# Cross attention with quads of heads: the previous head's last weighing first, its value load ahead of GpSimd's maximum, and the second value product of a quad handled one step later

## What is computed

```python
q = (layernorm(x) @ Wq).reshape(b, sq, 16, 128) / sqrt(128)   # sq = 256
k = (ctx @ Wk).reshape(b, 4096, 16, 128)
v = (ctx @ Wv).reshape(b, 4096, 16, 128)
attn = softmax(einsum('bqhd,bkhd->bhqk', q, k), axis=-1)
x = x + einsum('bhqk,bkhd->bqhd', attn, v).reshape(b, sq, 2048) @ Wo
```

## Time and profile before

| what | value |
|---|---|
| median of 3 runs | 1631.89 us (1631.61 to 1635.02) |
| profiled execution: its own time | 1632.26 us |
| its span, first to last instruction | 1630.4 us |
| PE busy | 1595.6 us (98%) |
| DVE busy | 1175.9 us (72%) |
| ACT busy | 728.2 us (45%) |
| cross attention, about | the first 1155 us |

### The profile page before, as it was taken

The page is one execution under the profiler, slowest core; times in us unless marked ns, Lnnn a source line. Parts: engine busy times, 40 slices in busy tenths (PEclk is TensorE's granted clock), DMA queues, the critical chain, the costliest instruction groups (busy, mean ns, idle before and its releaser), DMA issues. The chain is left out here.

```text
span 1630.4 us, 23096 instructions
## 1 busy us (share of the span) xinstructions
PE 1595.6 (98%) x8798; PEld 1255.8 (77%) x8798; DVE 1175.9 (72%) x2127; ACT 728.2 (45%) x981; POOL 192.5 (12%) x247
## 2 busy tenths in 40 slices
PE   9999999999999999989999999998999999999998
PEld 7887888888788888878888888887757757544544
DVE  5555888888788888878888889999583762633333
ACT  4334554555455555544555556565331351322221
POOL 0001011010100101010110101111100071011110
PEclk9999999999999999999999999999999999999999
DMA  7876555564655655554455444334320517489994
GB/s 237 228 228 191 156 148 148 145 162 124 176 145 148 154 144 156 124 167 133 133 135 134 134 120 123 104 116 138 128 102 30 206 52 309 179 262 416 424 423 171
DMA packets 125661, 283.48 MB, mean 174 GB/s; under 512 B 7729, under 2 KB 83697, under 8 KB 119409
## 3 DMA queue, kind: packets, MB, share of 16 engines
q1 hardware_dynamic: 103248, 201.27, 38.1%
q0 software_dynamic: 22304, 80.75, 17.8%
HBM read 207.51 MB, written 74.48 MB: 173 GB/s over the span
## 5 line engine op out<-in xcount | busy, mean ns | idle before, releaser
L502 PE MATMUL bank<-wv_parts,cT_hi 128*128 128x512 f32 x1024 | 334.4, 390 | 1.0 <-DMA wv_parts<-wv_dram 1.0
L502 PEld LDWEIGHTS bank<-wv_parts,cT_hi 128*128 128x128 f32 x1024 | 192.8, 188 | 41.3 <-DMA wv_parts<-wv_dram 1.4
L470 PE MATMUL bank<-cT_hi,wk_hi 128*128 128x512 f32 x512 | 201.2, 393 | 0.6 <-DVE cT_lo L858 0.6
L470 PE MATMUL bank<-cT_lo,wk_hi 128*128 128x512 f32 x512 | 200.0, 391 | 0.0
L502 PE MATMUL bank<-wv_parts,cT_lo 128*128 128x512 f32 x512 | 199.8, 390 | 0.0
L470 PE MATMUL bank<-cT_hi,wk_lo 128*128 128x512 f32 x512 | 199.8, 390 | 0.0
L704 ACT CAST e_parts<-S 128x1024 fp32r<-128x1024 f32 (+1 forms) x129 | 134.9, 1045 | 139.7 <-PE bank L526 133.9
L964 DVE TENSOR_TENSOR e_parts<-S,e_parts 128x1024 fp32r<-128x1024 f32 (+1 forms) x129 | 156.0, 1209 | 40.6 <-ACT e_parts L704 37.7
L695 ACT ACTIVATE S<-S 128x1024 f32<-128x1024 f32 (+1 forms) x129 | 136.0, 1055 | 103.4 <-DVE S L930 101.3
L881 DVE TENSOR_TENSOR mx<-mx,S 128x256 f32<-128x256 f32 x390 | 165.3, 424 | 18.4 <-ACT S L689 8.1
L930 DVE TENSOR_TENSOR S<-S,mrow 128x1024 f32<-128x1024 f32 (+1 forms) x129 | 162.2, 1258 | 4.7 <-POOL mrow L1205 4.6
(11 more groups left out here) (328 smaller groups left out, 2793.7 us busy)
## 6 DMA issues: line engine op xcount, KB each, us to landing
w<-in_w_moe SPq DMA_DIRECT2D x32, 2304.0 KB, 15.4
v_dram<-v_out SPq DMA_DIRECT2D x112, 512.0 KB, 4.7
v_back<-v_dram POOLq DMA_DIRECT2D x110, 512.0 KB, 4.6
ctx_nat<-in_ctx SPq DMA_DIRECT2D x8, 1024.0 KB, 5.4
ctx_raw<-in_ctxT SPq DMA_DIRECT2D x7, 1024.0 KB, 8.9
v_dram<-v_back SPq DMA_DIRECT2D x14, 512.0 KB, 4.9
v_late<-v_dram POOLq DMA_DIRECT2D x14, 512.0 KB, 3.7
wv_parts<-wv_dram POOLq DMA_DIRECT2D x6, 1024.0 KB, 8.2
```

The source lines that it names most:

```text
L470: t = e.matmul(banks[b][:], l, r, start=(c == 0 and m == 0), stop=(c == DT - 1 and m == 2))
L502: t = e.matmul(banks[b][:], l, r, start=(c == 0 and m == 0), stop=(c == DT - 1 and m == 2))
```

## The change

It has four parts.

1. TensorE: in heads 4 and 8, step 0, `weigh(h-1, 7)` stands ahead of `project_k(h+1, 0)`, as in the other heads. GpSimd: in the same place `load_v` is issued ahead of `largest_score`.
2. ACT, DVE and SP: in the first head of each quad (0, 4 and 8) the second of step 1's two value units is rounded, subtracted and written at step 2, ahead of step 2's own. TensorE projects it where it did.
3. Heads 12 and 13: the weights of the queries are rounded and subtracted before those of the keys.
4. Head 14, step 6: `split_e` of the last chunk stands ahead of `keep_max` on DVE.

```diff
+        def moved_units(h, j):
+
+            if h < LATE and starts_quad(h) and j in (1, 2):
+                pair = units(h, 1)
+                return pair[:1] if j == 1 else pair[1:] + units(h, 2)
+            return units(h, j)
...
-                    for u in units(h, j):
+                    for u in moved_units(h, j):
                         spill(u)
...
-                    elif j == 0 and h and not starts_quad(h):
+                    elif j == 0 and h:
                         weigh(h - 1, NCH - 1)
                     project_k(h + 1, j)
-                    if j == 0 and h and starts_quad(h):
-                        weigh(h - 1, NCH - 1)
...
-                    for u in units(h, j):
+                    for u in moved_units(h, j):
                         round_v(u)
...
                     if j + 1 == NCH - 1 and h + 2 < XH:
+                        round_qo("wq", h + 2)
                         round_wk(h + 2)
-                        round_qo("wq", h + 2)
...
-                for u in units(h, 1):
+                for u in moved_units(h, 1):
                     split_v(u)
...
-                    for u in units(h, j):
+                    for u in moved_units(h, j):
                         split_v(u)
...
+                    if j == NCH - 2 and h == XH - 2:
+                        split_e(h, j + 1)
                     keep_max(h + 1, j - 1)
                     if j + 1 < NCH:
-                        split_e(h, j + 1)
+                        if j < NCH - 2 or h < XH - 2:
+                            split_e(h, j + 1)
...
                     if j + 1 == NCH - 1 and h + 2 < XH:
+                        split_qo("wq", h + 2)
                         split_wk(h + 2)
-                        split_qo("wq", h + 2)
...
                     if h < LATE:
-                        if h and j == 0 and starts_quad(h):
-                            largest_score(h)
                         load_v(n)
...
-                    if h and j == 0 and n != TAIL and not (h < LATE and starts_quad(h)):
+                    if h and j == 0 and n != TAIL:
                         largest_score(h)
```

## The result

The changed kernel took 1639.32 us (median of 6 runs, 1637.06 to 1639.88), the kernel before 1631.95 us on the same chip (6 runs, 1631.19 to 1635.02). The ratio is 1.0038, with a 95% interval from 1.0028 to 1.0048: slower by 6.2 us by the ratio, by 7.4 by the medians. The prediction was 1635.6, with a range of 1629.0 to 1641.0. The direction and the range are right, and the middle is 3.7 us too low.

The account below looks back on a forecast made before the run. TensorE, busy 98% of the span, was taken as the bound. Terms: +5.6 (heads 4 and 8), 0 (head 0), 0 (values), -1.5 (clock), -0.4 (parts 3 and 4), sum +3.7, giving 1635.6 us, range 1629.0 to 1641.0.

Parts of the forecast that it names:

- Part 2's waits: Step 3: TensorE waits 3.0 us in heads 4 and 8, about 2 in head 0; net loss 5.6 in heads 4 and 8.
- Rival A: The moved unit's write is hidden, ACT's wait is off TensorE's path: faster, 1627.7 us; chance 0.13.
- rival C: Clock falls in step 3's new waits, heads 4 and 8, 1.6 us each: clearly slower, 1638.8 us; chance 0.20.
- nearer to 2.25: Head 8's start: 2.5 us of idleness is nearer to head 4's 2.25 than to 3.91, so the clock holds.
- Net 0: Head 0: the 1.81 us wait is won in step 2 and lost in step 3; up to 1.9 lost with a longer write.
- I take a gain of 0: Start of heads 4 and 8: earlier load of values wins 0 us; the other end is 2.9 for both.
- an earlier issue only lengthens the stay in the queue: Start of head 8: values issued up to 2.7 us earlier still land behind the weights, at 706.2.
- cannot pass: GpSimd's queue: descriptors start in order, so the values cannot pass the weights and the gain is 0.
- Bare waits: Step 0 of heads 4 and 8: TensorE stands 1.57 us before the scores, where it stood 0.15; cost 1.4.
- the clock at head 8's start: Idleness comes in two pieces, 1.6 and 2.5 us, so the clock holds: gain about 1.5 us (0 to 1.6).
- -0.4: Heads 12 to 14, parts 3 and 4: gain of 0.4 us of a possible 1.0, all from part 3; other end 0.
- rival B: Early load lands early, full value of part 1 (2.9 us): no change, 1632.7 us; chance 0.17.

Follow-up runs that it names:

- Run 5: Changed kernel with the moved value unit written twice, first to a spare place in memory; 1645.46 us, ratio 1.0084 against the kernel before.
- run 3: Changed kernel with the second unit rounded and subtracted at the head of step 2, behind the exponential parts; 1624.85 us, ratio 0.9965 against before.
- Run 1: Changed kernel without part 2, each value unit handled in the step that projects it; 1627.03 us, ratio 0.9975 against the kernel before.
- run 2: Kernel before with part 2 alone, the second value unit handled at step 2; 1644.25 us, ratio 1.0076 against the kernel before.
- run 4: Kernel before with only TensorE's order of part 1, GpSimd's maximum still ahead of the load; 1629.0 us, ratio 0.9989 against before.
- Run 6: Kernel before with TensorE's order of part 1, head 8's key weights loaded behind step 1's writes; 1627.1 us, ratio 0.9972 against before.
- run 9: Kernel before with only GpSimd's order of part 1, load of values ahead of the maximum; 1633.38 us, ratio 1.0006 against before.
- run 7: Kernel before with parts 3 and 4 alone; 1632.98 us, ratio 1.0004 against the kernel before.
- run 8: Changed kernel without parts 3 and 4, the second unit handled at the head of step 2; 1625.05 us, ratio 0.9953 against the kernel before.

## Why the prediction was right in direction and short in size

**Part 2's waits: right.** The working gave 3.0 us in heads 4 and 8 and 2.0 in head 0, and 2.71, 2.85 and 2.25 came. Its steps held one by one in head 4: a write of 3.7 (3.67), the third unit at 444.5 (446.62, of which some 2.0 had been lost earlier), 5.7 from there to the keys of step 3 (452.30 - 446.62 = 5.68). ACT stood 5.02 us before that unit, where I had said about 4. (438.4 + 1.8 + 0.7 is 440.9 and not 440.7, which changes nothing.) Run 5 shows that the write's length goes through to TensorE, run 3 that the wait goes with the place and not with the step. Rival A falls with them.

**The clock behind them: the step that failed.** The sum counts the waits of part 2 at their own length. The fall was priced, at 1.6 us each, but only as rival C and for two heads. In the profiled execution it came behind all three waits: +4.8 us, which is more than the whole miss of 3.7. For head 8's start I had taken it that 2.5 us of idleness is "nearer to 2.25" and holds the clock, and used the same row of head 4 for the waits of step 3. The length of one wait does not decide: in the changed kernel's head 0 the clock fell after 2.25 us, the very length after which it had held before. "Net 0" for head 0 failed for this reason: the wait was moved and became dearer. The 0.69 that rival C quotes after 3.4 us is the mean of a window in which the clock fell from 1.00 to 0.50 on the way, so it was as full a fall as the others.

**The values' landing: mis-sized in head 8.** "I take a gain of 0" stood on the queue being full from the issue on, though the rows show landings and not how full a queue is. In the changed kernel the start of head 8 came 2.3 us earlier, the bound that I had worked out from the exponential parts; in head 4 it came 0.2 earlier. Run 1 has 2.25 and 3.91 us of waiting turned into 1.40 and 0.24 each. The times from issue to landing, counted from the start of the weights' row in GpSimd's timeline, are these (us; head 4 / head 8):

| kernel | values issued | values landed |
|---|---|---|
| before | 7.2 / 7.0 | 13.3 / 15.0 |
| run 2 | 7.2 / 7.0 | 13.3 / 14.5 |
| run 4 | 5.7 / 5.7 | 12.7 / 14.6 |
| changed kernel | 4.4 / 4.3 | 13.2 / 12.4 |
| run 1 | 4.4 / 4.3 | 12.4 / 12.8 |
| run 3 | 4.4 / 4.3 | 12.5 / 12.5 |

The changed kernel's issues in heads 4 and 8, as in the earlier trace rows:

```profile
v_back<-v_dram POOLq DMA_DIRECT2D x1, 512.0 KB, 8.7
...
v_back<-v_dram POOLq DMA_DIRECT2D x1, 512.0 KB, 8.1
```

So "an earlier issue only lengthens the stay in the queue" was nearly true in head 4, where an issue 2.7 us earlier landed 0.2 to 1.0 earlier. It was false in head 8, where the same landed 2.3 to 2.6 earlier, while the first 1.3 us of it (run 4) won only 0.4. The rule of the Trainium skill that I had set beside it (DMA: Bandwidth & Descriptors, section Two DMAs through the same engine are not ordered: descriptors of one queue start in order) agrees with the changed kernel, where the second transfer of weights landed at about 708.0 us (issued at some 698.4, 9.6 us to landing) and the values at 710.1. But start order is all that the page gives; that the values "cannot pass" and so gain 0 was my own step. They never did pass: they landed behind the weights in every trace that has both landings. Yet the weights' landing was not fixed either: it came 10.3 us behind the start of their row in the changed kernel and 11.7 before, so the values could gain from behind them.

One difference in head 8 fits the jump. SyncE's key weights were issued 1.8 us or more ahead of the values in the kernel before and in runs 2 and 4, and landed ahead of them; in the changed kernel and in runs 1 and 3 they were issued within 0.4 us of the values and landed behind them. Run 6, with the key weights away, gained 0.9 us. That they hold the values back is a guess that fits; it is not shown.

It took both halves of part 1: TensorE's order lets go of the buffer sooner, which alone gave 0.6 us in head 4, 0.4 in head 8 and the clock (run 4), and GpSimd's order, which is worth nothing by itself (run 9), brought the rest in head 8.

**Bare waits and the clock at head 8's start: right.** TensorE stood 1.40 us before the scores of step 0 where 1.57 was expected. And 1.6 us were won on the clock against 1.5, though for another reason than argued, since the second wait was gone instead of 2.5 us long.

**Parts 3 and 4: mis-sized.** -0.4 should have been about 0: run 7 shows the 1.0 us in the wait for DVE's sums, which the prediction had named as the other end. The clock takes part here as well. In the changed kernel it had fallen before TensorE went on with the sums at 1135.09 and stayed low; before, TensorE worked at 1.00 for its first us there. Windows of before, then of the changed kernel:

```profile
1128.70:1129.70 1.00, 0.96 (x6) 0.75 (x7) 0.97 (x3) 0.12 (x2) 0.50 (x2) 1.00 0.00 0
...
1135.10:1136.10 1.00, 1.00 (x5) 1.00 (x6) 0.97 (x3) 0.14 (x1) 0.45 (x2) 0.50 0.00 0
```

From the sums to the end of the last weighing the same matmuls took 1.2 us longer than before (24.2 against 23.0). Run 1 waits as long for the sums (4.4 us) and has nothing of it, so the longer wait alone does not bring it.

The errors, then: clock behind step 3's waits +4.8, values -2.3, parts 3 and 4 and the end of the cross attention +1.3, the rest -0.1. The sum +3.7 was short by 3.7. That it lies in the range is in part luck: the misses of 4.8 and -2.3 us have opposite signs, and without the second the time would have been 1641.6, outside the range. Rival C was the nearest case (1638.8), and rival B was half true beside it.

**What stays open.** What makes the clock fall after one wait of some 2.2 us and not after another; whether SyncE's key weights lengthen the landing of the values (run 6); and whether parts 3 and 4 cost something (runs 7 and 8).

## What to carry to other kernels

When work with a write behind it and one buffer under it is moved to a later step, place it at the first point of that step where its engine is free, not in the step's usual place: the same write cost nothing early in the step and 2.3 to 2.9 us of TensorE's time, in each of three places, late in it. Price a new wait of 2 us or more on a TensorE that has no other slack once with and once without a fall of the clock; here the fall made 2.7 us into 4.3, though four waits of 2.08 to 2.49 us elsewhere had none. Where a load waits for a buffer, look for who can let go of the buffer sooner and check that nothing stands ahead of the issue; reordering the issuing queue alone gained nothing here. Then look at what else is in flight: 2.7 us of earlier issue bought 2.3 to 2.6 us in head 8 and 0.2 to 1.0 in head 4.

## What the runs showed of the hardware

The clock fell to 0.50 (1.2 GHz) after waits of 2.25 (head 0, changed kernel) and 2.20 us (head 4, run 2), and stayed at 1.00 after waits of 2.25 us (head 4, before, and again in run 7), 2.49 (head 4, run 9) and 2.08 (head 8, run 4). Run 9's windows behind its 2.49 us in head 4 and its 3.34 us in head 8 show both cases in one execution:

```profile
425.00:427.00 2.00, 2.00 (x10) 1.64 (x10) 2.00 (x3) 1.74 (x2) 0.56 (x1) 1.00 0.14 14
...
707.00:709.00 2.00, 2.00 (x6) 1.52 (x6) 0.66 (x2) 1.63 (x2) 0.56 (x1) 0.50 0.07 23
```

The wait of 3.34 us is followed by 0.50, that of 2.49 is not. All six waits of step 3 that I read (three in the changed kernel, three in run 2, 2.09 to 2.85 us, before the scores) came with a fall, four behind the wait and two in its last us. The four that held were all waits for values at the start of a head, as was the one of 2.20 us that fell. What tells the two kinds apart was not tried. Each trace shows one execution, and the number of falls seems to differ between executions. The kernel's time goes with this clock: the six runs of run 2 reach from 1637.06 us, with a mean clock of 0.996 over the span, to 1646.44 with 0.991.
